# First layer's normalization: of the two images that VectorE normalizes for each chunk, ScalarE takes one

## What is computed

```python
def _gn(v, G=32, eps=1e-5):
    g = v.reshape(B_, H_, W_, G, C_ // G)
    m = jnp.mean(g, axis=(1, 2, 4), keepdims=True)
    s = jnp.var(g, axis=(1, 2, 4), keepdims=True)
    return ((g - m) / jnp.sqrt(s + eps)).reshape(v.shape)

x = x + _L0_conv_ref(_gn(x), ...)   # lambda layer: q, k, v products, softmax of k, relative positions
x = x + _L1_conv_ref(_gn(x), ...)   # two masked attentions
x = x + _L2_conv_ref(_gn(x), ...)   # attention with relative positions
x = x + _L3_conv_ref(_gn(x), ...)   # tensor-train channel product and 3x3 convolution
```

## Time and profile before

| what | value |
|---|---|
| time, median of 3 runs | 1200.97 us (1199.74 to 1202.2) |
| time of the profiled execution | 1200.26 us |
| its span | 1198.4 us |
| TensorE (PE) busy | 1177.1 us, 98% |
| VectorE (DVE) busy | 634.6 us, 53% |
| ScalarE (ACT) busy | 463.7 us, 39% |
| GpSimd (POOL) busy | 669.3 us, 56% |
| the first 54 us: PE, DVE, ACT, POOL busy | 41.29, 42.01, 25.50, 31.57 us |
| granted TensorE clock, mean | 0.999 |

### The profile page before, as it was taken

How to read it: one execution, slowest core, us unless ns; L and a number is a source line. 1 busy time by engine, 2 the same in 40 slices (tenths; PEclk the granted TensorE clock), 3 DMA queues, 4 the chain that set the end, 5 groups by cost and what they waited for, 6 DMA issues and landing times.

```text
span 1198.4 us, 18684 instructions
## 1 busy us (share of the span) xinstructions
PE 1177.1 (98%) x6304; PEld 949.0 (79%) x6304; DVE 634.6 (53%) x1546; ACT 463.7 (39%) x1197; POOL 669.3 (56%) x759
## 2 busy tenths in 40 slices
PE   6999999999999999999999999999999999999998
PEld 4788897468888888888888888787788878777887
DVE  7624352785564533464545367675436767468212
ACT  3520232035465530265633045554304655444212
POOL 4733379446667556667655656665565666563000
PEclk9999999999999999999999999999999999999999
DMA  6211114014766664466678357887835788730112
GB/s 192 86 45 45 44 29 127 24 43 129 215 191 188 184 176 142 113 192 182 196 189 221 114 148 214 227 237 215 234 115 144 217 225 233 217 95 1 36 36 71
DMA packets 184479, 171.78 MB, mean 143 GB/s; under 512 B 64192, under 2 KB 135520, under 8 KB 184384
## 3 DMA queue, kind: packets, MB, share of 16 engines
q1 hardware_dynamic: 148736, 163.70, 47.0%
q10 hardware_dynamic: 35648, 6.89, 3.0%
HBM read 120.20 MB, written 46.14 MB: 139 GB/s over the span
## 4 chain that ended last, share of the span: by engine, by line
PE 91%; DVE 3%; DMA 3%; POOL 1%; SPq 1%; issue 1%; ACT 0%; ACTq 0%; POOLq 0%; DVEq 0%
PE PS L1135 56%; PE PS L1782 7%; PE PS L682 7%; PE PS L1177 4%; PE PS L960 3%; PE PS L969 2%; PE PS L975 2%; PE PS L1198 2%; PE PS L1209 2%; PE PS L1799 2%; PE PS L665 1%; DVE part L1755 1%; PE PS L1225 1%; DMA w_raw<-in_w 1%; DMA turned<-part 1%
## 5 line engine op out<-in xcount | busy, mean ns | idle before, releaser
L1135 PE MATMUL PS<-XB,w_hi 128*128 128x512 f32 x1024 | 333.6, 393 | 1.3 <-POOL w_lo L228 1.3
L226 POOL CAST w_hi<-w_raw 128x512 fp32r<-128x512 f32 x195 | 120.6, 619 | 264.1 <-PE PS L1135 185.3
L228 POOL TENSOR_TENSOR w_lo<-w_raw,w_hi 128x512 fp32r<-128x512 f32 x195 | 251.4, 1289 | 15.6
L1135 PEld LDWEIGHTS PS<-XB,w_hi 128*128 128x128 f32 x1024 | 192.2, 188 | 45.0 <-issue 2.3
L1348 ACT ACTIVATE part<-PS,nmax 128x256 f32<-128x256 f32 (+1 forms) x256 | 112.1, 443 | 240.5 <-DVE nmax L1468 146.9
L1135 PE MATMUL PS<-XB,w_lo 128*128 128x512 f32 x512 | 199.7, 390 | 0.0
L1135 PE MATMUL PS<-XB,part 128*128 128x512 f32 x768 | 187.1, 391 | 0.0
L1135 PEld LDWEIGHTS PS<-XB,part 128*128 128x128 f32 x768 | 143.5, 188 | 30.9
L228 POOL TENSOR_TENSOR part<-part,part 128x512 fp32r<-128x512 f32 x85 | 109.5, 1288 | 6.8
L1135 PEld LDWEIGHTS PS<-XB,w_lo 128*128 128x128 f32 x512 | 96.2, 188 | 19.6 <-issue 0.2
L1358 ACT ACTIVATE part<-part,prec 128x256 f32<-128x256 f32 (+1 forms) x256 | 105.7, 475 | 14.7 <-DVE prec L1484 14.7
(11 more groups left out here) (137 smaller groups left out, 1764.3 us busy)
## 6 DMA issues: line engine op xcount, KB each, us to landing
w_raw<-in_w SPq DMA_DIRECT2D x187, 256.0 KB, 2.9
part<-in_w SPq DMA_DIRECT2D x85, 256.0 KB, 3.1
part<-turned SPq DMA_DIRECT2D x32, 512.0 KB, 5.3
turned<-part SPq DMA_DIRECT2D x60, 256.0 KB, 4.3
turned<-part SPq DMA_DIRECT2D x64, 192.0 KB, 3.5
part<-turned SPq DMA_DIRECT2D x32, 384.0 KB, 4.6
values<-part SPq DMA_DIRECT2D x128, 64.0 KB, 2.8
part<-values SPq DMA_DIRECT2D x32, 256.0 KB, 4.4
```

Source lines behind the costliest of these rows:

```text
L226: pool.tensor_copy(hi, raw).then_inc(w_hi_done, 1)
L228: pool.tensor_tensor(lo, raw, hi.bitcast(F32), ALU.subtract).then_inc(w_ready, 1)
L1135: m = nc.tensor.matmul(PS[:, bank, :], wt[:, (c % 4) * P:(c % 4) * P + P], rhs(hl, c), start=c == k == 0, stop=c == CK - 1 and k == 2)
```

## The change

Of `y`, ScalarE does images 1, 2 and 3 in this order, and VectorE image 0. A new semaphore `y_one` is raised by ScalarE's activation for image 1; VectorE's `rest` waits for it besides its own `y`. The waits that guard the two buffers of `ytmp` follow: VectorE's `y` waits for `lo[0]` as before, ScalarE's `y` for `lo[0]` and `lo[1]`.

```diff
+                self.y_one = sem("gn_y_one")
...
                 if c >= 2:
-                    eng.wait_ge(self.lo[h], c - 1)
-                for b in (2 * h, 2 * h + 1):
+                    eng.wait_ge(self.lo[0], c - 1)
+                    if h:
+                        eng.wait_ge(self.lo[1], c - 1)
+                for b in (1, 2, 3) if h else (0,):
                     k = c * B + b
                     dst, src = ytmp[:, c % 2, b * N:(b + 1) * N], xT[:, c, b * N:(b + 1) * N]
                     scale, shift = coef[:, i, 0, k:k + 1], coef[:, i, 1, k:k + 1]
                     if h:
                         last = nc.scalar.activation(dst, src, ACT.Identity, bias=shift, scale=scale)
+                        if b == 1:
+                            last.then_inc(self.y_one, 1)
                     else:
                         last = nc.vector.tensor_scalar(dst, src, scale, shift, ALU.mult, ALU.add)
                 last.then_inc(self.y_act if h else self.y_dve, 1)
...
                 eng.wait_ge(self.y_act if h else self.y_dve, c + 1)
+                if not h:
+                    eng.wait_ge(self.y_one, c + 1)
                 eng.wait_ge(self.hi, 2 * c + h + 1)
```

## The result

| | before | changed |
|---|---|---|
| median | 1200.97 us (1199.74 to 1205.12, 21 runs) | 1202.9 us (1201.32 to 1206.13, 21 runs) |
| ratio, 95% interval | | 1.0015 [1.0008, 1.0022] |
| profiled execution, its span | 1200.26, 1198.4 us | 1205.38, 1203.4 us |

The change makes the kernel 0.15% slower, 1.9 us by the medians. It was timed twice more beside other kernels: 1.0013 [1.0004, 1.0023] and 1.0017 [1.0008, 1.0026]. All three are under the 0.2% that counts as no change here, and all three intervals lie above 1.

What follows compares the result with a forecast made beforehand. TensorE, busy 98%, bounds the kernel; the question was when chunk 5's half 1 gets its high part. GpSimd's late `power(4)` gives +1.34 us, nothing gained: 1200.97 + 1.34 = 1202.3 us, range 1200.3 to 1204.4.

Steps and rivals of the forecast that it cites:

- The wait at chunk 1: VectorE's `rest(1)`, with nothing between it and `y(1)`, starts at 20.11 in place of 18.63: +1.48 us.
- VectorE catches up: Chunks 3 and 4: blocked time on VectorE goes, so `rest(4)` starts at 38.39 in place of 38.19, only +0.20 us.
- GpSimd's order is late next: Before `power(4)` GpSimd has `rest(4)` and `w_split(5)`, so `power(4)` starts near 42.35 in place of 41.01: +1.34 us.
- TensorE's own limit: Without a wait from chunk 3's to chunk 5's second matmul, TensorE arrives at 45.29; +0.97 us, the lower end.
- Chunk 6's weights: Split behind GpSimd's `rest(5)`, ready at 50.95, wanted at 51.0; 0.4 us of blocking gives the upper end, +1.7.
- The first rival: Before `coefficients(3)`, the widening copy falls behind GpSimd's subtraction, 1.3 us more: 1203.7 us, +0.22%; chance 0.15.
- Relief that reaches the end: VectorE's lost blocking removes all waits before the second matmuls: at the limit -2.4 us, 1198.6 us; chance 0.05.
- Given back later: A later TensorE wait not set in motion by TensorE absorbs up to 1.3 us: 1201.0 us; chance 0.11.

Runs made afterwards that it cites:

- the new orders: VectorE order y(1), groups(2), rest(1), coefficients(2), stats(3): on the kernel before, 26.53 us; with chunk 1 two and two and `power(4)` ahead of `w_split(5)`, 25.34 and 25.72 us.
- the better order: The change, with VectorE's order y(1), groups(2), rest(1), coefficients(2), stats(3): 25.54 us from `head(1)` to chunk 5's second matmul, ratio 0.9998 [0.9989, 1.0007].

## Why the prediction was right

The forecast was 1202.3 us in a range of 1200.3 to 1204.4 and within 0.2%; measured were 1202.9 and +0.15%. Step by step, times after `head(1)`:

| step | predicted | measured |
|---|---|---|
| chunk 1: `rest(1)` | 2.68 | 2.66 |
| chunk 2's second matmul | 9.85 (+1.48) | 9.82 |
| `rest(2)` | 10.39 | 10.35 |
| chunk 3's second matmul | 16.80 (+1.43) | 16.78 |
| `rest(3)` | 17.35 | 17.31 |
| `rest(4)` on VectorE | 20.96 (+0.20) | 20.89 |
| `power(4)` | 24.92 (+1.34) | 24.91 |
| chunk 5's second matmul | 28.23 (+1.34) | 28.22 |

The mechanism was right, step by step, and each step hits to less than 0.1 us.

- **The wait at chunk 1** costs, and it costs what is queued behind it: shown by putting back chunk 1 (26.76), by changing chunk 1 alone (28.35) and by taking `groups(2)` out from behind the wait (26.40).
- **VectorE catches up** in chunks 3 and 4 since its blocked time goes. Shown in the profile, by changing chunk 1 alone, where these chunks are as before and `rest(4)` comes 22.22 us after `head(1)` in place of 20.89, and by the version with `power(4)` first, where it was worth 0.41 us.
- **GpSimd's order is late next**, and TensorE's own limit behind it (27.86 by the prediction's sum, 27.81 measured with `power(4)` first).
- **Chunk 6's weights** were safer than the prediction had them. It let them fit by 0.05 us; measured, they were ready at 49.94 us and TensorE wanted them at 50.57. GpSimd's cast and subtraction took 0.61 and 1.29 us there, not the 1.07 and 1.42 of before, since VectorE stood idle when they began.
- **A sign that was named wrongly:** the prediction's list of signs has VectorE waiting some 2 us before `rest(2)` as well. It waited 0.19 us there, as the prediction's own working for chunk 2 says (`stats(4)` covers the rest).
- **The first rival** did not happen in the changed kernel: the copy at 31.07 took 0.16 us. Its mechanism is real, as the new orders showed at chunk 2.
- **Relief that reaches the end** did not happen; of the 5.7 us less of busy time on VectorE, 0.13 us reached chunk 5 (28.22 in place of the 28.35 with chunk 1 alone).
- **Given back later** is not seen: in each of the other thirteen profiles TensorE's distance from before's first one, whatever the first stage had made it (-2.4 to +0.9 us), stayed the same to 0.05 us from the first q matmul at 60 us to about 1020 us. No wait in between gives anything back or adds anything. After that the wait at 1022 us for L1511 of the earlier trace rows (1.3 us in before, from 0.2 to 1.6 in the others) and the loads near 1038 and 1053 us blur it, by up to 1.7 us, and by 3.4 in the first profile of the change.

**What the prediction lacked** is a cost at the other end of the kernel. The medians are 1.9, 2.2 and 2.3 us apart where the stage gives 1.33. From the end of TensorE's last matmul to the end of the span it is 4.16 and 4.17 us in the two profiles of before, and 4.88, 4.93 and 4.89 in the three of the change, with every instruction between them as before. What differs is the last write of the output. From the view of the transfers, first before from 1195.75 us to the end, then changed from 1200.02 us to the end (the last number of a write is us from issue to landing):

```profile
out_x<-xT SPq DMA_DIRECT2D x1, 256.0 KB, 2.1
```

```profile
q14 instruction: 1, 0.01, 0.9%
out_x<-xT SPq DMA_DIRECT2D x1, 256.0 KB, 2.8
```

In the change a packet of 8 KB, of the kind that the profile calls `instruction`, travels during that write, and the last ten packets of the write come one after another behind it. The fourteen profiles divide without exception: with such a packet in the last write, 4.88 to 5.05 us from TensorE's last matmul to the end (the three of the change, `power(4)` first, and the two orders with `groups(2)` first that keep three images in chunk 1); without it, 4.16 to 4.20 us (all others). With 0.7 us of it, the change should be 2.05 us slower, where 1.9, 2.2 and 2.3 were measured, and the better order 0.6 us faster, where 0.7 was measured. For the other versions, stage and end together come within 0.6 us of the medians too. So the second cost of the change lies in the last write; the stretch between differs by over 3 us from profile to profile, so it can't exclude a further few tenths. No run was made to move that packet, so its part is read from the traces and not shown by an experiment, and what decides when it comes is open. The prediction had no term for it: its forecast of 1202.3 is right for the stage, and 0.6 us low for the kernel by this.

## What to carry to other kernels

Moving an instruction to an idle engine helps only if the new hand-over is no later than the old one. Here, at chunk 1, 0.33 us of work left VectorE, and its wait before `rest(1)` grew from 0.46 to 2.25 us, since ScalarE had four other activations first. Ask what stands behind the new wait on that engine: where it was covered by statistics (chunk 0, chunk 2) or given back by blocked time (chunk 3) it was nearly free, where it wasn't (chunk 1) it cost its full 1.46 us, and a change of order of two lines removed it.

With VectorE and GpSimd both at work, a shift of a tenth of a microsecond can turn an instruction of 0.17 us into one of 1.26 us: the widening copy took 0.17 where it began 0.05 us ahead of GpSimd's subtraction, and 1.26 where it began 0.06 us behind it. So a reordering has to be worked out instruction by instruction, and its profile read for durations that doubled, not only for waits.

When the medians of a change differ steadily by more than the changed stage explains, look at the very end of the kernel too, behind the last instruction of the engine that bounds it. A comparison that stops at TensorE's last matmul could not see the 0.7 us here.

## What the runs showed of the hardware

After the wait of 1.99 us near 1054 us in one profile of the changed kernel, TensorE ran eight matmuls of 128x256 in 1.08 us, as before; then its matmuls of 128x512 began 0.43 us apart, eight of them from 1055.76 on (the rows above show the first), in place of 0.23 us. That is the pace of its lower clock, 1.2 GHz, against 2.4 GHz, and the granted clock of the stretch from 1055.70 to 1059.30 us is 0.53 in that profile, where it is 1.00 in before's. It cost 1.6 us, nearly as much again as the wait. In the thirteen other profiles the pace did not fall there, with waits of up to 1.70 us at the same place (chunk 1 alone).

One `instruction` packet of 8 KB during a write of 256 KB made the write land in 2.8 to 3.0 us in six profiles, in place of 2.1 to 2.2 in the eight without it.
